# Shared network of a routed FFN in groups of four tiles: weights as the stationary operand of its first layer

## The chip, the cores and the metric

One core of a Trainium2 chip runs the kernel. The time is that of one execution on the device in microseconds (us), from the runs listed below. Five engines work side by side and meet at semaphores: the tensor engine (PE in the rows, PEld its weight loads), the vector engine (DVE), the scalar engine (ACT), GpSimd (POOL) and the sync engine (SP), which here only issues transfers. Each engine executes its own instructions in the order in which they are written.

## What is computed

The input is 64 x 64 rows of 512 values, 4096 tokens, seen as 32 tiles of 128. Each batch entry picks one of 8 matrices by a subject number; after that each token goes to 4 of 16 experts and to a shared network of the same form. Cut to what matters:

```
h      = einsum('bct,bcd->bdt', x, weights[subjects]) + bias[subjects]   # (64, 64, 512)
scores = sigmoid(h @ gate_weight.T)               # 16 experts, groups of 4, two best groups
w, sel = top 4 of the biased scores in those groups, weights normalised, times 2.5
out    = sum over the 4 experts of w * (silu(h @ g.T) * (h @ u.T)) @ d.T
shared = (silu(h @ shared_gate.T) * (h @ shared_up.T)) @ shared_down.T
return x + out + shared                           # H = 512, I = 256, float32
```

## The kernel before

**Stages.** A first stage, up to about 54 us, makes h, transposes it into kept_w and x_ring, computes the router's logits and starts the routing arithmetic. The shared stage then runs the shared network over the 32 tiles (steps 0 to 31); meanwhile the vector engine works out who goes where. The routed stage runs 143 tiles of gathered tokens (steps 32 to 174), each with one expert's weights, partly in loops of 16 steps. NT is 32, the first routed step.

**A step.** Products are made in float32 precision from two parts each, a high part rounded to the tensor engine's format and the low rest: three matmuls for each of four (first layer) or two (second layer) blocks of 128. In step n the tensor engine makes the first-layer product of tile n (`gate_up`, 12 matmuls of 512 columns, x stationary, the weights moving, gate and up side by side in one bank of psGU), transposes hid of tile n-1 (`xpose_hid`, 2 transposes to psH), and makes the second-layer product of tile n-2 (`down`, 6 matmuls to psY). Line 937 issues all the matmuls of products, line 814 all transposes.

The scalar engine copies y of tile n-3 (line 724), the high part of x of tile n+1 (`copy_xT`, 662), makes silu (772) and the high part of the transposed hid (717). The vector engine subtracts for the low part of x (`split_x`, 1385), multiplies silu and up (`mix`, 1408) and splits hid (1398).

**What lies between.** In the shared stage the vector engine carries pieces of the routing arithmetic, one or two for each step by the table ROUTE_STEPS (0 groups, 1 best groups, 2 top experts, 3 ties, 4 counts, ... 22 fill_idx), and the table entries by ENTRY_STEPS (16 entries in steps 10 to 20), which the scalar engine scales (`scale_lanes`, 757) and the tensor engine adds up in psM (`fill_slots`, 963, in the step behind). The tensor engine also makes a counting product in step 5 and word tables in step 14. HIGHS and LOWS say in which step the next experts' weights are split; GATHERS after which y the first gathers go out on GpSimd; RAW_LOADS the loads of weights.

The x of the shared stage is kept transposed. `shared_tile(n)` is the tile of step n, in x_ring for the first eight steps, in kept_w after them.

**The routed stage.** Steps 32 and on take x by gather, shuffle and a vector transpose (1392), two steps ahead. The vector and sync engines loop from step 48, the tensor and scalar engines from 46; DVE_HEAD fixes where the vector engine's loop body is loaded, and ACT_STEPS adds 52 semaphore instructions ahead of the scalar engine's code, which moves its loop body.

The functions that the diff touches follow.

## Time and profile before

| | us |
|---|---|
| median of 3 runs | 847.3 (845.91 to 850.49) |
| profiled execution | 847.83 |
| its span, first to last instruction | 846.1 |
| tensor engine busy | 824.8 (97%) |
| vector, scalar engine, GpSimd busy | 488.6 (58%), 406.9 (48%), 437.8 (52%) |
| granted clock of the tensor engine, mean | 0.995 |

A row of a timeline gives start, duration, engine, line, operation, what is written from what, shapes and a count; in brackets stands the idle time ahead of it and what ended that. Matmuls overlap, so what a matmul costs in a queue is the distance of the starts, not its duration.

### The profile page before, as it was taken

What the parts mean: (1) busy time and instruction counts of PE and PEld (TensorE: products, weight loads), DVE (VectorE), ACT (ScalarE), POOL (GpSimd) and SP (SyncE); (2) the same over time, 40 slices, a digit from 0 to 9 for tenths busy, and PEclk for the clock granted to TensorE, in tenths of its full rate; (3) what the DMA queues carried; (4) which work ended last, traced back from release to release, by engine and by line L of the source; (5) the groups of instructions that cost most, each with busy time, mean ns of one, the idle gap of its engine ahead of it and who ended that gap; (6) DMA issues with size and microseconds to landing.
All of it is one profiled execution on the core that took longest, in us unless ns stands there. A gap on an engine that the chain in (4) does not pass through costs nothing.

```text
span 846.1 us, 19696 instructions
## 1 busy us (share of the span) xinstructions
PE 824.8 (97%) x4200; PEld 660.7 (78%) x4201; DVE 488.6 (58%) x1016; ACT 406.9 (48%) x849; POOL 437.8 (52%) x400
## 2 busy tenths in 40 slices
PE   8999999999999999999999999999999999999994
PEld 5568878788888888788888888888888887887883
DVE  5688875645654455754457546646556566464441
ACT  4763457645444435534446435546455354453341
POOL 5403111265366556467565666655565675766433
PEclk9999999999999999999999999999999999999998
DMA  8977958599999999799997999798998998998744
GB/s 319 400 270 224 198 101 240 102 268 233 244 272 212 173 198 181 163 292 252 192 182 154 284 238 214 192 283 179 239 267 200 270 245 213 244 194 185 138 64 64
DMA packets 145307, 181.54 MB, mean 215 GB/s; under 512 B 30570, under 2 KB 103922, under 8 KB 142834
## 3 DMA queue, kind: packets, MB, share of 16 engines
q0 software_dynamic: 37776, 89.08, 51.7%
q1 hardware_dynamic: 106528, 80.45, 35.5%
q10 hardware_dynamic: 834, 10.49, 3.4%
q14 instruction: 151, 1.24, 0.5%
q8 instruction: 18, 0.29, 0.1%
HBM read 82.52 MB, written 67.17 MB: 177 GB/s over the span
## 4 chain that ended last, share of the span: by engine, by line
PE 85%; DMA 4%; DVE 3%; issue 3%; ACT 3%; DVEq 1%; ACTq 0%; SPq 0%; POOL 0%
PE psGU L937 53%; PE psY L937 26%; PE psH L814 4%; DMA h_rows<-tok_ring 3%; DVE xT_lo L1385 1%; ACT x_ring L757 1%; PE psM L963 1%; ACT tok_ring L670 1%; ACT xT_hi L662 0%; DVE x_ring L1367 0%; POOL out L594 0%; ACT y_ring L724 0%; DVEq L1490 0%; DMA cond_sb<-cond_w 0%; ACT x_ring L677 0%
## 5 line engine op out<-in xcount | busy, mean ns | idle before, releaser
L937 PE MATMUL psGU<-split_w,xT_hi 128*128 (+1 forms) x1400 | 433.9, 391 | 1.3 <-DVE xT_lo L1385 0.9
L594 POOL DMA_INDIRECT out<-y_ring,idx_all x143 | 235.3, 1646 | 207.4 <-SPq L485 189.4
L937 PEld LDWEIGHTS psGU<-split_w,xT_hi 128*128 128x128 f32 x1400 | 262.4, 188 | 59.1 <-issue 2.2
L937 PE MATMUL psGU<-split_w,xT_lo 128*128 (+1 forms) x700 | 273.8, 391 | 0.0
L937 PE MATMUL psY<-split_w,hidT_hi 128*128 (+1 forms) x700 | 233.2, 414 | 0.2 <-issue 0.2
L772 ACT ACTIVATE aT<-psGU 128x256 f32<-128x256 f32 x175 | 67.1, 384 | 263.6 <-PE psGU L937 208.8
L589 POOL DMA_INDIRECT tok_ring<-h_rows,idx_all x143 | 148.3, 1037 | 59.3 <-issue 43.1
L1385 DVE TENSOR_TENSOR xT_lo<-psT,xT_hi 128x512 fp32r<-128x512 f32 x143 | 98.7, 690 | 135.7 <-ACT xT_hi L662 101.3
L724 ACT ACTIVATE y_ring<-psY 128x512 f32<-128x512 f32 x174 | 103.1, 593 | 115.1 <-PE psY L937 88.6
L937 PEld LDWEIGHTS psGU<-split_w,xT_lo 128*128 128x128 f32 x700 | 131.4, 188 | 29.5
L937 PE MATMUL psY<-split_w,hidT_lo 128*128 (+1 forms) x350 | 138.2, 395 | 0.0
L937 PEld LDWEIGHTS psY<-split_w,hidT_hi 128*128 128x128 f32 x700 | 118.4, 189 | 17.0 <-issue 0.5
L1410 DVE SCALAR_TENSOR_TENSOR aT<-aT,w_ring,psGU 128x256 f32<-128x256 f32 x143 | 67.0, 468 | 93.9 <-ACT aT L772 65.4
L1392 DVE STREAM_TRANSPOSE psT<-x_ring 128x512 f32<-128x512 f32 x143 | 102.5, 717 | 4.6 <-issue 4.6
L602 POOL DMA_DIRECT2D out<-y_ring x32 | 29.1, 922 | 112.8 <-ACT y_ring L724 112.4
L662 ACT ACTIVATE xT_hi<-psT 128x512 fp32r<-128x512 f32 x143 | 84.8, 593 | 2.1 <-DVE psT L1392 2.1
L937 PEld LDWEIGHTS psY<-split_w,hidT_lo 128*128 128x128 f32 x350 | 65.6, 187 | 15.4
L1425 DVE TENSOR_TENSOR split_w<-raw_w,split_w x42 | 51.4, 1225 | 42.6 <-ACT split_w L734 29.2
L1398 DVE TENSOR_TENSOR hidT_lo<-psH,hidT_hi 128x256 fp32r<-128x256 f32 x175 | 72.7, 416 | 0.3
L814 PE MATMUL psH<-ident,aT 128*128 128x128 f32 x350 | 66.7, 272 | 1.3 <-DVE hidT_lo L1398 1.1
L814 PEld LDWEIGHTS psH<-ident,aT 128*128 128x128 f32 x350 | 48.0, 139 | 25.2 <-DVE aT L1410 1.6
L717 ACT ACTIVATE hidT_hi<-psH 128x256 fp32r<-128x256 f32 x175 | 66.5, 380 | 2.1 <-PE psH L814 1.7
(189 smaller groups left out, 403.4 us busy)
## 6 DMA issues: line engine op xcount, KB each, us to landing
x_ring<-tok_ring SPq DMA_DIRECT2D x284, 128.0 KB
raw_w<-ffn_w SPq DMA_DIRECT2D x17, 1536.0 KB, 10.4
h_rows<-tok_ring SPq DMA_DIRECT2D x32, 256.0 KB, 9.0
out<-y_ring POOLq DMA_DIRECT2D x32, 256.0 KB
x_ring<-x_pairs SPq DMA_DIRECT2D x12, 512.0 KB, 9.2
tok_ring<-h_rows,idx_all POOLq DMA_INDIRECT x143
out<-y_ring,idx_all POOLq DMA_INDIRECT x143
h_rows<-zeros POOLq DMA_DIRECT2D x1, 2112.0 KB, 9.1
```

What stands on the lines that cost most here:

```text
L589: pool.indirect_dma_start(tok_ring[:, r % RING, :], None, h_rows[:, :], bass.IndirectOffsetOnAxis(idx_all[:, r:r + 1], 0)).then_inc(gather ...
L594: pool.indirect_dma_start(out[:, :], bass.IndirectOffsetOnAxis(idx_all[:, r:r + 1], 0), y_ring[:, r % YRING, :], None, compute_op=ALU.add) ...
L662: act.activation(xT_hi[:, t.slot % 2, :], xT, ACT.Copy).then_inc(xhi_ready, 1)
L717: act.activation(hidT_hi[:, t.slot % 2, :], psH[:, 0:I], ACT.Copy).then_inc(hidhi_ready, 1)
L724: act.activation(y_ring[:, s, :], psY[t.slot % 2][:], ACT.Copy).then_inc(y_ready, 1)
L772: act.activation(silu[:, t.slot % 2, :], psGU[t.slot % 2][:, 0:I], ACT.Silu).then_inc(silu_ready, 1)
L814: mm = pe.transpose(dst[:, k * P:(k + 1) * P], src[:, k * P:(k + 1) * P], ident[:])
L937: mm = pe.matmul(dst, a[:, slot, c], w(at + col + k * H), start=(k == 0 and a is high and at == 0), stop=(k == parts - 1 and a is low))
L1385: v.tensor_tensor(xT_lo[:, t.slot % 2, :], xT, xT_hi[:, t.slot % 2, :].bitcast(F32), ALU.subtract).then_inc(xT_ready, 1)
L1392: v.transpose(psT[t.slot % 2][:].rearrange("p (k b j) -> p k j b", k=HK, j=QUADS), x_duo[:, t.slot // DUO_TILES, :, t.slot % DUO_TILES, :] ...
L1398: v.tensor_tensor(hidT_lo[:, t.slot % 2, :], psH[:, 0:I], hidT_hi[:, t.slot % 2, :].bitcast(F32), ALU.subtract).then_inc(hidT_ready, 1)
L1410: ins = v.scalar_tensor_tensor(out=hid[:, half, :], in0=gate, scalar=w_ring[:, w_slot, bass.ds(expert, 1)], in1=up, op0=ALU.mult, op1=ALU. ...
```

## The change

The shared stage runs in eight groups of four tiles. For one half c of the 256 inner columns (gate, then up) a product (`shared_product`) takes 128 columns of the weights as stationary operand and the four tiles' x as moving operand, four runs of 128 columns, so that hid comes out transposed, [inner, token]: 12 matmuls of 512 columns, gate to psGU[0], up to psGU[1], four products per group. Silu, mix, the high copy and the split of hid work on 512 columns for a half and four tiles. The second layer stays as it was, tile by tile (`shared_down`), one group behind. hid is not transposed there.

Buffers are found in others: high parts of x of a group in xT_pair, tok_ring or entry; low parts of x replace x in x_ring and kept_w; hid in aT and ties. New waits keep these apart (on gu_done for entries and gathers, on table_done and h_stored for copies). Steps 0 to 31 are written out ahead of the loops. The table of gathers, HIGHS and LOWS move; the padding on the scalar engine goes; in the routed stage the scalar engine copies y at the end of a step instead of at its start.

```diff
 KEPT_ORDER = [k * (KEPT // 2) + 2 * j + i for j in range(PIECES) for k in range(2) for i in range(2)]
-HIGHS = {18: (1, 0), 19: (1, 1), 20: (1, 2), 24: (2, 0), 28: (2, 1), 31: (2, 2)}
-LOWS = {21: ((1, 0),), 23: ((1, 1),), 24: ((1, 2),), 26: ((2, 0),), 29: ((2, 1),), 31: ((2, 2),)}
+HIGHS = {18: (1, 0), 19: (1, 1), 21: (1, 2), 25: (2, 0), 29: (2, 1), NT: (2, 2)}
+LOWS = {21: (1, 0), 23: (1, 1), 24: (1, 2), 26: (2, 0), 30: (2, 1), NT: (2, 2)}
+GROUP = 4
 RAW_LOADS = {15: 1, 16: 2, 23: 3, 31: 4}
 WARM_UP = 8
 DVE_HEAD = 77
...
 WEIGHTS_STORE = 3
-FIRST_GATHER = 20
-GATHERS = {20: (0, 1), 21: (2, 3), 22: (4, 5), 23: (6, 7), 25: (8, 9), 26: (10, 11), 27: (12, 13)}
+FIRST_GATHER = 18
+GATHERS = {18: (0, 1), 19: (2, 3, 4, 5), 20: (6, 7), 21: (8, 9), 22: (10, 11), 23: (12, 13)}
 
 
...
         aT = sb("aT", [P, 2, H])
-        xT_hi = sb("xT_hi", [P, 2, H], F32R)
-        xT_lo = sb("xT_lo", [P, 2, H], F32R)
+        xT_pair = sb("xT_pair", [P, GROUP, H], F32R)
+        xT_hi, xT_lo = xT_pair[:, 0:2, :], xT_pair[:, 2:4, :]
         silu, hid = aT[:, :, 0:I], aT[:, :, I:2 * I]
...
                 for r in GATHERS.get(n, ()):
+                    if r == RING - GROUP:
+                        pool.wait_ge(gu_done, NT - 2 * GROUP)
                     gather(r)
...
-            for _ in range(ACT_STEPS):
-                act.sem_inc(act_clear, 1)
...
+            def copy_shared_xT(n):
+
+                g, j = divmod(n, GROUP)
+                if n <= GROUP:
+                    act.wait_ge(a_xT_ready, NT if n == GROUP else shared_tile(n) + 1)
+                if n == GROUP:
+                    for k in range(RING - GROUP, RING):
+                        act.wait_ge(h_stored[k], 16 * (NT // RING))
+                if g >= 2 and j == 0:
+                    act.wait_ge(gu_done, GROUP * (g - 1))
+                if n == NT - GROUP:
+                    act.wait_ge(table_done, N_GROUPS)
+                act.activation(group_high(g)[:, j, :], kept_xT(shared_tile(n)), ACT.Copy).then_inc(xhi_ready, 1)
 
...
+            def shared_silu(g, c):
+
+                act.wait_ge(gu_done, GROUP * g + 2 * c + 1)
+                if c == 1 and g > 0:
+                    act.wait_ge(down_done, GROUP * g)
+                elif c == 0 and g > 1:
+                    act.wait_ge(down_done, GROUP * (g - 1))
+                act.activation(shared_hid(g, c), psGU[0][:], ACT.Silu).then_inc(silu_ready, 2)
+
+            def shared_hid_highs(g, c):
+
+                act.wait_ge(hid_ready, GROUP * g + 2 * c + 2)
+                act.activation(shared_hid_high(g, c), shared_hid(g, c), ACT.Copy).then_inc(hidhi_ready, 2)
+
...
+            def split_ahead(n):
+
+                turn, j = HIGHS[n]
+                if j == 0:
+                    act.wait_ge(raw_loaded, 16 * turn)
+                act.wait_ge(gu_done, KEPT_IN_X + (turn - 1) * KEPT + (j + 1) * GROUP)
+                split_high(turn, j)
+
+            def shared_step(n):
+
+                g, part = divmod(n, GROUP)
+                if part == 0 and g > 0:
+                    shared_hid_highs(g - 1, 1)
+                if n + GROUP < NT:
+                    copy_shared_xT(n + GROUP)
+                elif n == NT - 1:
+                    copy_xT(tile_at(NT), NT)
+                if part == 0:
+                    shared_silu(g, 0)
+                elif part == 1:
+                    shared_hid_highs(g, 0)
+                    if g > 0:
+                        shared_y(g - 1, 0)
+                elif part == 2 and g > 0:
+                    for j in range(1, GROUP):
+                        shared_y(g - 1, j)
+                for e in ENTRY_STEPS.get(n, ()):
+                    scale_lanes(e)
+                if part == 3:
+                    shared_silu(g, 1)
+                if n in HIGHS:
+                    split_ahead(n)
+                if n in X_COPIES:
+                    copy_x(X_COPIES[n])
 
             def next_weights(t, word):
...
             def step(t, n, j):
-                if n is None or n >= 3:
-                    copy_y(t + -3, None if n is None else n - 3)
-                if n is None or 0 < n < LAST:
+                if n == NT:
+                    shared_hid_highs(NT // GROUP - 1, 1)
+                if n is None or n < LAST:
                     copy_xT(t + 1, None if n is None else n + 1)
                 if n == NT:
                     act.wait_ge(words_ready, 1)
-                if not is_shared(n):
-                    word = act.value_load(act_word[0:1, bass.ds(t.done(-NT), 1)])
+                word = act.value_load(act_word[0:1, bass.ds(t.done(-NT), 1)])
                 act.wait_ge(gu_done, t.done(1))
-                if n is None or n >= 2:
-                    act.wait_ge(hid_ready, t.done(-1))
+                act.wait_ge(hid_ready, t.done(-1))
                 act.activation(silu[:, t.slot % 2, :], psGU[t.slot % 2][:, 0:I], ACT.Silu
                                ).then_inc(silu_ready, 1)
-                if n != 0:
+                if n == NT:
+                    for k in range(GROUP):
+                        shared_y(NT // GROUP - 1, k)
+                    split_ahead(NT)
+                else:
                     copy_hidT(t + -1, None if n is None else n - 1)
-                for g in ENTRY_STEPS.get(n, ()):
-                    scale_lanes(g)
-                if not is_shared(n):
-                    next_weights(t, word)
-                elif n in HIGHS:
-                    turn, j = HIGHS[n]
-                    if j == 0:
-                        act.wait_ge(raw_loaded, 16 * turn)
-                    act.wait_ge(xT_ready, KEPT_IN_X + (turn - 1) * KEPT + (j + 1) * (KEPT // PIECES))
-                    split_high(turn, j)
-                if n in X_COPIES:
-                    copy_x(X_COPIES[n])
+                    if n is None or n >= NT + 3:
+                        copy_y(t + -3, None if n is None else n - 3)
+                next_weights(t, word)
 
             act.activation(warm[:], ones[:, 0:1], ACT.Silu)
+            for n in range(NT):
+                shared_step(n)
             run_tiles(act, *FFN, step)
...
+            def shared_product(g, c, up):
+
+                col = up * I + c * P
+                for k in range(HK):
+                    high, low = group_high(g)[:, :, k * P:(k + 1) * P], group_low(g, k)
+                    in_four = psGU[up][:].rearrange("p (t q) -> p t q", q=P)
+                    as_low = in_four if len(low.shape) == 3 else psGU[up][:].rearrange("p (a i q) -> p a i q", a=2, q=P)
+                    w = k * H + col
+                    pe.matmul(in_four, split_w[:, w:w + P], high, start=(k == 0), stop=False)
+                    pe.matmul(as_low, split_w[:, w:w + P], low, start=False, stop=False)
+                    mm = pe.matmul(in_four, split_w[:, EW + w:EW + w + P], high, start=False, stop=(k == HK - 1))
+                return mm
+
+            def shared_down(g, j):
+
+                n = GROUP * g + j
                 if j == 0:
-                    kept.clear()
-                if n == NT:
-                    pe.wait_ge(words_ready, 1)
-                elif n == 1:
-                    pe.wait_ge(scored, LOGIT_GROUPS)
-                at, needed = weights(t, n)
-                kept.append(at)
-                gate_up(t, n, kept[-1], needed)
-                if n != 0:
-                    xpose_hid(t + -1, None if n is None else n - 1)
+                    pe.wait_ge(hidT_ready, GROUP * (g + 1))
+                if n >= 2:
+                    pe.wait_ge(y_ready, n - 1)
+                token = slice(j * P, (j + 1) * P)
+                for c in range(IK):
+                    low = shared_hid_low(g, c)
+                    for a, at in ((shared_hid_high(g, c), 0), (shared_hid_high(g, c), EW), (low, 0)):
+                        w = at + UP + c * H
+                        mm = pe.matmul(psY[n % 2][:], a[:, token], split_w[:, w:w + H], start=(c == 0 and a is not low and at == 0),
+                                       stop=(c == IK - 1 and a is low))
+                mm.then_inc(down_done, 1)
+
+            def shared_step(n):
+
+                g, part = divmod(n, GROUP)
+                if part == 0:
+                    pe.wait_ge(xT_ready, GROUP * (g + 1))
+                    if g > 0:
+                        pe.wait_ge(silu_ready, GROUP * g)
+                    shared_product(g, 0, 0).then_inc(gu_done, 1)
+                elif part == 1:
+                    if g > 0:
+                        pe.wait_ge(hid_ready, GROUP * g)
+                    shared_product(g, 0, 1).then_inc(gu_done, 1)
+                    if g > 0:
+                        shared_down(g - 1, 0)
+                elif part == 2:
+                    if g > 0:
+                        for j in range(1, GROUP):
+                            shared_down(g - 1, j)
+                else:
+                    pe.wait_ge(silu_ready, GROUP * g + 2)
+                    shared_product(g, 1, 0).then_inc(gu_done, 1)
+                    pe.wait_ge(hid_ready, GROUP * g + 2)
+                    shared_product(g, 1, 1).then_inc(gu_done, 1)
                 if n in PE_POS_FFN:
                     positions(PE_POS_FFN[n])
                 elif n == PE_WORDS:
                     word_tables()
                 elif n == PE_SP_WORDS:
                     sp_table()
-                if is_shared(n):
-                    for g in ENTRY_STEPS.get(n - 1, ()):
-                        fill_slots(g)
-                if n is None or n >= 2:
+                for e in ENTRY_STEPS.get(n - 1, ()):
+                    fill_slots(e)
+
+            pe.wait_ge(h_ready, NT)
+            pe.wait_ge(low_done, PIECES)
+            for n in range(NT):
+                shared_step(n)
+            pe.wait_ge(scored, LOGIT_GROUPS)
+            pe.sem_inc(hid_xposed, NT)
+            pe.wait_ge(words_ready, 1)
+            kept = []
+
+            def step(t, n, j):
+                if j == 0:
+                    kept.clear()
+                at, needed = weights(t, n)
+                kept.append(at)
+                gate_up(t, n, kept[-1], needed)
+                if n == NT:
+                    for k in range(GROUP):
+                        shared_down(NT // GROUP - 1, k)
+                else:
+                    xpose_hid(t + -1, None if n is None else n - 1)
+                if n is None or n >= NT + 2:
                     down(t + -2, None if n is None else n - 2,
...
+            def split_shared_x(n):
+
+                g, j = divmod(n, GROUP)
+                if n == 0:
+                    v.wait_ge(logits_done, LOGIT_GROUPS - 1)
+                elif n == GROUP:
+                    v.wait_ge(logits_done, LOGIT_GROUPS)
+                v.wait_ge(xhi_ready, n + 1)
+                tile = shared_tile(n)
+                v.tensor_tensor(low_xT(tile), kept_xT(tile), group_high(g)[:, j, :].bitcast(F32),
+                                ALU.subtract).then_inc(xT_ready, 1)
+
+            def shared_mix(g, c):
+
+                v.wait_ge(silu_ready, GROUP * g + 2 * c + 2)
+                v.wait_ge(gu_done, GROUP * g + 2 * c + 2)
+                hid_c = shared_hid(g, c)
+                v.tensor_tensor(hid_c, hid_c, psGU[1][:], ALU.mult).then_inc(hid_ready, 2)
+
+            def split_shared_hid(g, c):
+
+                v.wait_ge(hidhi_ready, GROUP * g + 2 * c + 2)
+                hid_c = shared_hid(g, c)
+                v.tensor_tensor(shared_hid_low(g, c), hid_c, shared_hid_high(g, c).bitcast(F32), ALU.subtract
+                                ).then_inc(hidT_ready, 2)
+
+            def shared_step(n):
+
+                g, part = divmod(n, GROUP)
+                if part == 0 and g > 0:
+                    shared_mix(g - 1, 1)
+                elif part == 2:
+                    split_shared_hid(g, 0)
+                    if g < NT // GROUP - 1:
+                        split_shared_x(GROUP * (g + 1))
+                route_part(n)
+                if part == 0 and g > 0:
+                    split_shared_hid(g - 1, 1)
+                elif part == 1:
+                    shared_mix(g, 0)
+                elif part >= 2 and g < NT // GROUP - 1:
+                    for j in ((1,) if part == 2 else (2, 3)):
+                        split_shared_x(GROUP * (g + 1) + j)
+                if n in LOWS:
+                    split_low(*LOWS[n])
+                if n == NT - 2:
+                    turn_x(tile_at(NT))
+                elif n == NT - 1:
+                    split_x(tile_at(NT))
+                    turn_x(tile_at(NT + 1))
...
-            split_x(tile_at(0), 0)
+            for n in range(GROUP):
+                split_shared_x(n)
             route_weights(0)
             def copy_y(t):
```

**On the vector engine**, between best groups and ties of the routing arithmetic. `aT` takes mix, `hidT_lo` or `aT_low` the split of hid, `xT_lo` or `x_low` the split of x, MAX is top experts. Before:

```order
L1408 TENSOR_TENSOR aT<-aT,psGU 128x256
L1398 TENSOR_TENSOR hidT_lo<-psH,hidT_hi 128x256
L1385 TENSOR_TENSOR xT_lo<-x_ring,xT_hi 128x512
L1120 MAX top<-masked 128x8 x16
L1019 TENSOR_TENSOR ties<-masked,top 128x16x16
```

Now:

```order
L1576 TENSOR_TENSOR aT<-aT,psGU 128x512
L1582 TENSOR_TENSOR aT_low<-aT,hidT_hi 128x512
L1568 TENSOR_TENSOR x_low<-x_ring,tok_high 128x512
L1290 MAX top<-masked 128x8 x16
L1189 TENSOR_TENSOR ties<-masked,top 128x16x16
```

Mix and split of hid now serve four tiles and stand once in two steps; the splits of x that the next group needs (tiles 4 to 7) stand one here, one behind top experts and two behind ties.

**On the tensor engine**, where a first-layer product is followed by a second-layer one (before: steps 2 and 3; now: steps 4 and 5). `psGU` is the first layer, `psY` the second, `psH` the transposed hid. Before:

```order
L937 MATMUL psGU<-split_w,xT_lo 128x512
L814 MATMUL psH<-ident,aT 128x128 x2
L937 MATMUL psY<-split_w,hidT_hi 128x512 x2
L937 MATMUL psY<-split_w,hidT_lo 128x512
L937 MATMUL psY<-split_w,hidT_hi 128x512 x2
```

Now:

```order
L1091 MATMUL psGU<-x_low,split_w 128x512
L1092 MATMUL psGU<-tok_high,split_w 128x512
L1107 MATMUL psY<-split_w,hidT_hi 128x512 x2
L1107 MATMUL psY<-split_w,aT_low 128x512
L1107 MATMUL psY<-split_w,hidT_lo 128x512 x2
```

The two transposes are gone, and x has become the moving operand of psGU; the product to psY has the six matmuls that it had.

**On the scalar engine**, around the first table entries (steps 10 and 11). L757 and L876 are the scaling of entries. Before:

```order
L662 ACTIVATE xT_hi<-kept_w 128x512
L772 ACTIVATE aT<-psGU 128x256
L717 ACTIVATE hidT_hi<-psH 128x256
L757 ACTIVATE x_ring<-x_ring,token_no 128x512 x2
L724 ACTIVATE y_ring<-psY 128x512
```

Now:

```order
L790 ACTIVATE y_ring<-psY 128x512 x3
L876 ACTIVATE x_ring<-x_ring,token_no 128x512 x2
L727 ACTIVATE tok_high<-kept_w 128x512
L876 ACTIVATE x_ring<-x_ring,token_no 128x512 x2
L799 ACTIVATE aT<-psGU 128x512
```

Three copies of y stand together, and a silu of the group (L799) stands behind two scalings of entries.

## Rows read from the trace of the kernel before

**Rows 1.** The page: busy time by engine, and the group of the transposes.

```profile
PE 824.8 (97%) x4200; PEld 660.7 (78%) x4201; DVE 488.6 (58%) x1016; ACT 406.9 (48%) x849; POOL 437.8 (52%) x400
...
L814 PE MATMUL psH<-ident,aT 128*128 128x128 f32 x350 | 66.7, 272 | 1.3 <-DVE hidT_lo L1398 1.1
```

**Rows 2.** Timeline, tensor engine: stage's start, one step, first routed products.

```profile
54.25 0.70 PE L937 MATMUL psGU<-split_w,xT_hi 128*128 128x512 f32 x2
...
62.92 0.71 PE L937 MATMUL psY<-split_w,hidT_hi 128*128 128x512 f32 x2
...
64.39 0.62 PE L937 MATMUL psGU<-split_w,xT_hi 128*128 128x512 f32 x2
...
67.13 0.38 PE L814 MATMUL psH<-ident,aT 128*128 128x128 f32 x2
67.27 0.71 PE L937 MATMUL psY<-split_w,hidT_hi 128*128 128x512 f32 x2
...
205.70 0.62 PE L937 MATMUL psGU<-split_w,xT_hi 128*128 x2
...
214.41 0.62 PE L937 MATMUL psGU<-split_w,xT_hi 128*128 x2
```

**Rows 3.** Tensor engine: first matmuls of steps 5, 6, 14, 15, 19, 20.

```profile
73.10 0.62 PE L937 MATMUL psGU<-split_w,xT_hi 128*128 128x512 f32 x2
...
78.53 0.62 PE L937 MATMUL psGU<-split_w,xT_hi 128*128 128x512 f32 x2
...
116.05 0.62 PE L937 MATMUL psGU<-split_w,xT_hi 128*128 128x512 f32 x2
...
122.76 0.62 PE L937 MATMUL psGU<-split_w,xT_hi 128*128 128x512 f32 x2
...
144.61 0.62 PE L937 MATMUL psGU<-split_w,xT_hi 128*128 128x512 f32 x2
...
150.03 0.62 PE L937 MATMUL psGU<-split_w,xT_hi 128*128 128x512 f32 x2
```

**Rows 4.** Timeline, vector engine: route weights, groups and best groups.

```profile
51.65 0.42 DVE L1019 TENSOR_TENSOR w_num<-raw_w,scores 128x256 f32<-128x256 f32 x1
...
53.72 0.68 DVE L1385 TENSOR_TENSOR xT_lo<-x_ring,xT_hi 128x512 fp32r<-128x512 f32 x1
54.78 0.43 DVE L1019 TENSOR_TENSOR masked<-scores,ebias 128x256 f32<-128x256 f32 x1 [0.38 <-ACT scores L682]
...
56.02 0.55 DVE L1097 TENSOR_REDUCE group_sum<-raw_w 128x64 f32<-128x384 f32 x1
...
58.83 0.41 DVE L1019 TENSOR_TENSOR beats<-group_sum 128x48 f32<-128x48 f32 x3
...
61.21 0.42 DVE L1408 TENSOR_TENSOR aT<-aT,psGU 128x256 f32<-128x256 f32 x1
```

**Rows 5.** Timeline, vector engine: a split of x, top experts and ties.

```profile
61.88 0.68 DVE L1385 TENSOR_TENSOR xT_lo<-x_ring,xT_hi 128x512 fp32r<-128x512 f32 x1
62.48 1.32 DVE L1120 MAX8 top<-masked 128x8 f32<-128x16 f32 x16
...
65.35 0.42 DVE L1408 TENSOR_TENSOR aT<-aT,psGU 128x256 f32<-128x256 f32 x1
...
66.62 1.33 DVE L1019 TENSOR_TENSOR ties<-ties 128x256 f32<-128x256 f32 x3
...
69.37 0.42 DVE L1408 TENSOR_TENSOR aT<-aT,psGU 128x256 f32<-128x256 f32 x1
```

**Rows 6.** Timeline, scalar engine: copies of x, scalings, a routed step's silu.

```profile
50.31 1.15 ACT L662 ACTIVATE xT_hi<-x_ring 128x512 fp32r<-128x512 f32 x2 [0.27 <-issue]
...
143.57 2.61 ACT L757 ACTIVATE x_ring<-x_ring,token_no 128x512 f16<-128x512 f16 x4 [0.79 <-DVE x_ring L1367]
...
771.27 0.38 ACT L772 ACTIVATE aT<-psGU 128x256 f32<-128x256 f32 x1 [1.66 <-PE psGU L937]
```

**Rows 7.** Timeline, vector engine, where its loop ends.

```profile
779.25 0.73 DVE L1392 STREAM_TRANSPOSE psT<-x_ring 128x512 f32<-128x512 f32 x1 [4.56 <-issue]
```

133 lines of the change are left out of this document (84 added, 49 removed).

## The prediction

> **What bounds the kernel now.** I read the page first, then the tensor engine's instructions in order of time, then the vector and scalar engines over the same stretch. The tensor engine is busy for 824.8 of 846.1 us and no other engine for more than 58% [rows 1]. So a microsecond is gained only where the tensor engine executes less or waits less, and lost where it waits more. The profiled execution took 847.83 us, 0.5 above the median of 847.3; sums are made against it and 0.5 is taken off at the end.
>
> The change touches the shared stage: from the first product at 54.25 us to the first routed product at 205.70, and the two steps behind it, where the last second-layer products of the stage drain [rows 2]. By 214.41 both orders have done the same work: 34 first-layer products, 32 second-layer products. I compare how long that takes, 160.16 us now.
>
> A plain step [rows 2] is a first-layer product (12 matmuls, 64.39 to 67.13 = 2.74), a pair of transposes of hid (0.14), and a second-layer product (6 matmuls, 62.92 to 64.39 = 1.47), 4.35 from 62.92 to 67.27. The other work sits between steps, priced as a step's period less 4.35 [rows 3]: second counting product 5.43 - 4.35 = 1.08; word tables 6.71 - 4.35 = 2.36 (I take 2.3); two table fills 5.42 - 4.35 = 1.07, so 0.56 for one. There are 16 fills, 6 pairs and 4 single (8.7); the small word table I put at 0.6. Sum 12.6.
>
> **Part 1, transposes removed.** 64 transposes in 32 pairs. The page lists them at 272 ns each [rows 1], but that is latency. A pair advances the queue 0.14, and the second-layer product behind it begins with 0.55 for two matmuls instead of 0.46, hence 1.47 instead of 1.38. So a pair is worth 4.35 - 2.74 - 1.38 = 0.23, and 32 pairs 7.4 us. By the Trainium skill, page TensorE: Matmul & The Clock Gate, section Part 4: PE-mode transpose, a 128x128 transpose takes about 275 ns in a kernel; the trace's duration agrees (272), but as time in the queue that would be 64 x 0.275 = 17.6 us, and the spacing here says 7.4. I use the spacing.
>
> **Part 2, the first layer turned round.** Per group of four tiles 4 products of 12 matmuls of 512 columns: 48, as before. The moving operand is now four runs of 128 columns instead of one of 512. No row shows this form for these types. The nearest, the table fills, move every second f16 element of 144, 16 matmuls in 1.07 us [rows 3], 67 ns each with their transitions, or 0.46 ns per column against 227 / 512 = 0.44 for plain ones. I take zero; 384 matmuls make 1.9 us of each 5 ns, above only, since nothing in a gather of runs can be quicker than a plain stream.
>
> **Part 3, vector and scalar work.** The same elements in half as many instructions for hid (512 wide). A 512-wide vector operation advances its queue 0.60 (61.88 to 62.48) [rows 5], a 512-wide scalar one 0.53 (two in 1.15 less the tail) [rows 6]. That is cheaper in total than before, and off the bound. What is not off it is where these instructions stand: a group cannot start until all four of its tiles are split, where before one split sufficed, and the routing arithmetic is still queued between them in the same places.
>
> I walk the queues group by group with those prices; a group of the tensor engine is 4 x 2.74 + 4 x 1.38 = 16.48.
>
> Start: two more scalar copies (0.53 each) fit before the last logits copy, and the fourth split stands about where the second stands now, 53.72 to 54.40 [rows 4]; I let the first product start at 54.5 (+0.25).
>
> Group 0 has no second layer: 10.96, ready for group 1 at 65.5. The vector queue from 54.4 [rows 4, 5]: route weights 2.07 (51.65 to 53.72), groups 1.79 (54.78 to 56.57), best groups 2.38 (58.83 to 61.21), mix 0.61, a 0.85 wait for the scalar copy of hid (0.62 = 1.15 - 0.53 [rows 6], the tail of mix and the signals), split of hid 0.61, split of tile 4 0.60, top experts 2.87 (62.48 to 65.35), split of tile 5 0.60, ties 2.75 (66.62 to 69.37), splits of tiles 6 and 7 1.2. Sum 16.4: the queue reaches the end at 70.8. Group 1 starts at 70.9: **a wait of 5.4 us**, the largest new term. Before, the same arithmetic lay inside four steps of which each needed one split.
>
> Group 1 ends at 70.9 + 16.48 + 1.08 = 88.5. By the same kind of sum its splits for group 2 end 0.9 ahead of that, those for group 3 only 0.4 ahead. The further waits are estimates, each between zero and one piece of routing arithmetic (2.87 [rows 5]), and I name what is late. In group 2 the third second-layer product needs a bank of y whose copy stands, on the scalar engine, behind the copy of hid, which waits for mix, which stands behind top slots on the vector engine: 0.7. At its end the silu stands behind the scaling of a late table entry: 0.4. So group 2 ends at 88.5 + 16.48 + 0.7 + 0.56 (a fill) = 106.2 and group 3 starts at 106.6. Group 3: + 16.48 + two single fills and a pair 2.19 + word tables 2.3 + 0.6 = 128.2. Group 4: + 16.48 + a single fill and three pairs 3.77, and four scalings in 2.61 [rows 6] stand ahead of the copies of y (0.6) and again of the last silu (0.4): group 5 starts at 149.4 and ends, + 16.48 + two pairs 2.14, at 168.0. Groups 6 and 7 have nothing beside them: 201.0. Then the first routed product, four second-layer products, the second routed product and its transposes, 2.74 + 5.52 + 2.74 + 0.23 = 11.23, and a wait of 0.8, since the next tile's high copy stands behind four copies of y and a weight split: 213.0.
>
> Sum: 213.0 against 214.41, a gain of 1.4. Put otherwise: 7.4 from the transposes; the present stage holds 160.16 - (34 x 2.74 + 32 x 1.38 + 33 x 0.23 + 12.6) = 2.7 of waits that mostly go, because second-layer products now cover the fills; less 8.3 of new waits and 0.25 at the start; rounding makes the rest. From there the routed stage runs the same loops at 4.35 a tile [rows 2], so the gain is carried to the end: 847.8 - 1.4 = 846.4, less 0.5: **845.9 us**. The gathers move two tiles earlier in the table; the tensor engine does not wait for them now, and the first transposes that need them stand at step 30, 40 us behind. I put them at nothing; without that cover a gather and its shuffle would show.
>
> **Rivals.**
> 1. The vector queue does not hold up group 1 (less than half of the waits come true). For it: the rows' spacings include small waits between dependent operations, and a margin of one microsecond decides several of the smaller terms. Against: 16.4 us of listed work against 10.96. With no new wait at all: 846.4 - 8.3 - 0.5 = 837.6; with half, 841.7.
> 2. Slower: the routed loops. The change takes 52 padding instructions off the scalar engine's stream and many real ones from it, so its loop body lies elsewhere; the vector engine's loop keeps its fixed place. What a badly placed jump costs is seen on the vector engine: 4.56 us of idle with nothing to wait for, where its loop ends [rows 7]. The scalar engine has 1.66 us in hand in each step [rows 6], so it decides from a stall above that. Such a stall at loop entry and exit costs 2 x (4.56 - 1.66) = 5.8: 851.7; at all eight turns and the exit, 26, 872. By the Trainium skill, page Runtime: NRT & Kernel Launch, section Instruction fetch mechanics, a taken branch whose target is not in the two blocks held forces a fetch; the 4.56 us agrees with it, and no row tells where the new scalar loop falls.
> 3. Split matmuls slower: at 10% (23 ns) each, 384 x 0.023 = 8.8: 854.7. Against it the fills above. It would have to be above 4 ns to eat the forecast gain.
> 4. The longer queues make more waits than I walked: the splits for groups 2 and 3 come 0.9 and 0.4 us ahead only. Two more microseconds: 848.
>
> **How the numbers follow.** Forecast with its near neighbours (rival 4 too), 843 to 850: 0.65. Rival 1: 0.22. Rival 2: 0.09. Rival 3: 0.04. The forecast's time is the predicted one. The range takes in half of the way to rival 1's end and rival 2's smaller price: 839.5 to 851.5. A measurement tells 0.5%, 4.2 us, from no change: faster means below 843.1 (rival 1 and a little of the forecast's edge), slower above 851.5 (rivals 2 and 3).
>
> **What would show it.** The tensor engine idle for about 5 us before the second group's first product, waiting for the vector engine's split of x, shows the main term; its absence shows rival 1. The group's first product four times 2.74 after the start shows part 2; longer spacing rival 3. A period of 4.10 per tile in groups 6 and 7 shows part 1; 4.35 would mean that the transposes cost nothing. Idle time on the scalar engine above 1.7 us at the loop's turns shows rival 2. The forecast is wrong if the routing arithmetic on the vector engine is faster in the new order than its rows say, or if the routed stage's period is no longer 4.35.

## The result, and the profile after

The changed kernel takes 854.19 us (median of 19 runs, 852.70 to 858.74), the kernel before, run beside it, 848.80 (19 runs). The ratio is 1.0076, with a 95% interval of 1.0062 to 1.0091: slower by 5.4 us. The forecast was 845.9 and the range ended at 851.5. In the profiled executions the span grew from 846.1 to 851.8 us.

The page and the timeline of the tensor engine after, in groups that answer to [rows 1] and [rows 2]. The columns are those of the rows ahead; L1090 to L1092 are the three matmuls of a group's product, L1107 the second-layer products of the shared stage, L1049 the routed products.

```profile
span 851.8 us, 19349 instructions
PE 822.1 (97%) x4136; PEld 655.7 (77%) x4137; DVE 488.1 (57%) x984; ACT 391.8 (46%) x817; POOL 435.4 (51%) x400
```

```profile
54.29 0.47 PE L1090 MATMUL psGU<-xT_pair,split_w 128*128 128x512 f32 x1
...
65.06 0.39 PE L1092 MATMUL psGU<-xT_pair,split_w 128*128 128x512 f32 x1
70.70 0.80 PE L1090 MATMUL psGU<-tok_high,split_w 128*128 128x512 f32 x1 [5.26 <-DVE x_low L1568]
...
92.07 0.50 PE L1090 MATMUL psGU<-xT_pair,split_w 128*128 128x512 f32 x1 [0.93 <-DVE split_w L1568]
...
110.14 0.47 PE L1090 MATMUL psGU<-tok_high,split_w 128*128 128x512 f32 x1 [0.45 <-ACT aT L799]
132.04 0.48 PE L1090 MATMUL psGU<-xT_pair,split_w 128*128 128x512 f32 x1
...
205.41 2.92 PE L1049 MATMUL psGU<-split_w,xT_pair 128*128 x12
208.99 0.96 PE L1107 MATMUL psY<-split_w,ties_low 128*128 128x512 f32 x3 [0.65 <-DVE aT_low L1582]
220.69 3.01 PE L1049 MATMUL psGU<-split_w,xT_pair 128*128 x12 [2.92 <-DVE split_w L1642]
```

The tensor engine is busy 2.7 us less than in [rows 1] (822.1 against 824.8) and the span is 5.7 longer: it waits more. The piece of work that took 160.16 us in [rows 2], from the first product to the first-layer product of tile 34, now takes 220.69 - 54.29 = 166.40.

How the tensor engine's clock went around the first long wait. Each row is a stretch: its length, busy times and counts of PE, PEld, DVE, ACT and POOL, then the granted clock as a share of full speed, DMA share and GB/s.

```profile
60.00:65.40 5.40, 5.40 (x25) 4.17 (x23) 4.42 (x23) 2.25 (x4) 0.00 (x0) 1.00 0.53 194
65.40:70.70 5.30, 0.05 (x1) 0.00 (x0) 5.05 (x12) 0.00 (x0) 0.00 (x0) 0.86 0.00 0
70.70:76.00 5.30, 5.29 (x13) 4.14 (x14) 4.93 (x13) 1.15 (x2) 0.00 (x0) 0.50 0.00 0
76.00:81.50 5.50, 5.50 (x26) 4.57 (x25) 2.15 (x5) 2.73 (x5) 0.18 (x1) 1.00 0.00 0
```

During the 5.26 us of waiting the clock fell to one half (1.2 of 2.4 GHz), and the first 12 matmuls of group 1 ran at it: they took from 70.70 to 75.99, 5.29 us instead of 2.74. That cost 2.55 us in this execution, which no step of the prediction holds.

The second place is the end of the stage. The scalar engine, and then the vector engine, ahead of the wait of 2.92:

```profile
210.68 0.60 ACT L790 ACTIVATE y_ring<-psY 128x512 f32<-128x512 f32 x1 [1.92 <-PE psY L1107]
...
214.86 0.60 ACT L790 ACTIVATE y_ring<-psY 128x512 f32<-128x512 f32 x1 [0.80 <-PE psY L1107]
215.35 1.05 ACT L708 ACTIVATE split_w<-raw_w 128x1024 fp32r<-128x1024 f32 x1
216.30 1.05 ACT L853 ACTIVATE split_w<-raw_w  x1
217.26 0.58 ACT L713 ACTIVATE xT_pair<-psT 128x512 fp32r<-128x512 f32 x1
```

```profile
216.44 1.23 DVE L1244 TENSOR_TENSOR split_w<-raw_w,split_w 128x1024 fp32r<-128x1024 f32 x1 [6.52 <-ACT split_w L708]
218.60 1.23 DVE L1642 TENSOR_TENSOR split_w<-raw_w,split_w  x1 [0.94 <-DVE split_w L1244]
219.75 0.69 DVE L1556 TENSOR_TENSOR xT_pair<-psT,xT_pair 128x512 fp32r<-128x512 f32 x1
```

At step 32 the scalar engine writes the four y of group 7 first, each a second-layer product apart (210.68 to 214.86), and only then the high part of the last shared weight split (L708) and of the next expert's (L853). The vector engine's low parts (L1244, L1642) wait for these, and its split of x for tile 34 stands in its queue behind both: it starts at 219.75. The profile names L1642 as releaser; the product needs the split behind it.

**Where the 5.7 us went**, by the spans: the stage + 6.24; from the product of tile 34 to the scalar engine's last silu - 1.15 (614.10 against 615.25); from there to the issue of the last scatter + 1.25 (7.92 against 6.67); from that to the end - 0.63; the start + 0.04. The 1.15 is no merit of the change's products: in the kernel before, the routed step that starts at 777.03 takes 6.10 us instead of 4.35, behind the vector engine's standstill of 4.56 [rows 7], and after, where that standstill is 2.08, no step there is lengthened (one at 699.8 takes 5.72). The + 1.25 shows in these rows, first of the kernel after, then of before: the last copy of hid on the scalar engine comes 3.15 us after the instruction ahead of it, against 1.34.

```profile
839.09 0.38 ACT L783 ACTIVATE hidT_hi<-psH 128x256 fp32r<-128x256 f32 x1 [3.15 <-PE psY L1049]
```

```profile
831.66 0.38 ACT L717 ACTIVATE hidT_hi<-psH 128x256 fp32r<-128x256 f32 x1 [1.34 <-PE psH L814]
```

### The profile page after: what moved, and what is told of

Same layout as the page of the kernel before. It is cut to its first block, busy times and chain, and to the rows that moved or that the text cites. A ratio compares the mean times of both kernels' runs of the same rounds, so it can differ in the third digit from the quotient of the medians.

```text
span 851.8 us, 19349 instructions
## 1 busy us (share of the span) xinstructions
PE 822.1 (97%) x4136; PEld 655.7 (77%) x4137; DVE 488.1 (57%) x984; ACT 391.8 (46%) x817; POOL 435.4 (51%) x400
## 4 chain that ended last, share of the span: by engine, by line
PE 83%; DVE 2%; issue 1%; ACT 1%; ACTq 0%; DVEq 0%; POOL 0%; SPq 0%
PE psGU L1049 45%; PE psY L1049 23%; PE psH L928 4%; PE psY L1107 3%; PE psGU L1090 2%; PE psGU L1092 2%; PE psGU L1091 2%; PE psM L1077 1%; ACT x_ring L876 0%; DVE aT L1576 0%; PE psT L1013 0%; POOL out L650 0%; DVE entry L1537 0%; DVE aT_low L1582 0%; DVE split_w L1642 0%
## 5 line engine op out<-in xcount | busy, mean ns | idle before, releaser
L1049 PE MATMUL psGU<-split_w,xT_pair 128*128 x1716 | 415.9, 391 | 4.1 <-DVE split_w L1642 2.9
L1049 PEld LDWEIGHTS psGU<-split_w,xT_pair 128*128 128x128 f32 x1716 | 321.9, 188 | 75.1 <-issue 5.4
L1049 PE MATMUL psY<-split_w,hidT_hi 128*128 x572 | 190.6, 414 | 1.7 <-DVE hidT_lo L1620 1.5
L1556 DVE TENSOR_TENSOR xT_pair<-psT,xT_pair 128x512 fp32r<-128x512 f32 x143 | 98.8, 691 | 64.5 <-ACT xT_pair L713 49.0
L1049 PE MATMUL psY<-split_w,hidT_lo 128*128 x286 | 113.0, 395 | 0.0
L1049 PEld LDWEIGHTS psY<-split_w,hidT_hi 128*128 128x128 f32 x572 | 96.8, 189 | 15.9 <-issue 2.4
L713 ACT ACTIVATE xT_pair<-psT 128x512 fp32r<-128x512 f32 x143 | 86.5, 605 | 5.3 <-DVE psT L1614 3.1
L1642 DVE TENSOR_TENSOR split_w<-raw_w,split_w x42 | 51.5, 1226 | 43.4 <-ACT split_w L853 41.6
L1049 PEld LDWEIGHTS psY<-split_w,hidT_lo 128*128 128x128 f32 x286 | 53.6, 187 | 12.6
L1620 DVE TENSOR_TENSOR hidT_lo<-psH,hidT_hi 128x256 fp32r<-128x256 f32 x143 | 59.6, 417 | 2.4 <-ACT hidT_hi L783 2.4
L928 PE MATMUL psH<-ident,aT 128*128 128x128 f32 x286 | 54.4, 272 | 0.0
L853 ACT ACTIVATE split_w<-raw_w x42 | 44.8, 1066 | 0.9 <-issue 0.2
L1091 PE MATMUL psGU<-split_w 128*128 128x512 f32 x96 | 37.6, 391 | 0.0
```

Source lines behind the costliest of these rows:

```text
L713: act.activation(xT_hi[:, t.slot % 2, :], psT[t.slot % 2][:], ACT.Copy).then_inc(xhi_ready, 1)
L928: mm = pe.transpose(dst[:, k * P:(k + 1) * P], src[:, k * P:(k + 1) * P], ident[:])
L1049: mm = pe.matmul(dst, a[:, slot, c], w(at + col + k * H), start=(k == 0 and a is high and at == 0), stop=(k == parts - 1 and a is low))
L1091: pe.matmul(as_low, split_w[:, w:w + P], low, start=False, stop=False)
L1556: v.tensor_tensor(xT_lo[:, t.slot % 2, :], psT[t.slot % 2][:], xT_hi[:, t.slot % 2, :].bitcast(F32), ALU.subtract).then_inc(xT_ready, 1)
L1620: v.tensor_tensor(hidT_lo[:, t.slot % 2, :], psH[:, 0:I], hidT_hi[:, t.slot % 2, :].bitcast(F32), ALU.subtract).then_inc(hidT_ready, 1)
```

## The experiments

All are edits of the changed kernel unless said otherwise. "Stage" is the time from the first product to the product of tile 34: 160.16 before, 166.40 after. The medians of the kernel before in the runs' company were 848.5 to 848.8. The intervals of e1 to e6 and of e9 still meet that of the kernel after (1.0062 to 1.0091); for these the traces say more than the medians.

**e1: keep the tensor engine busy in the first wait.**

```
+                if n == GROUP:
+                    for k in range(23):
+                        pe.matmul(psY[0][:], split_w[:, 0:P], split_w[:, 0:H], start=True, stop=True)
```

> The changed kernel with 23 extra matmuls of 512 columns (5.2 us of work, results unused, into a bank of psY that is free then) on the tensor engine ahead of its wait for the first product of group 1. Theory (the wait for the vector engine's splits of x costs 5.3 us, and the tensor engine's clock, which fell to half behind it, costs another 2.6): the first product of group 1 starts at 70.7 as in the changed kernel, but with a granted clock of 1.00, so that its 12 matmuls are 0.23 apart instead of 0.43; the kernel is 2.6 us faster than the changed one, about 851.6. Rival (the loss lies in the routed stage, or in the form of the new matmuls): no change or slower, 854 and above.

Measured: 852.43 us, 1.0057 [1.0032, 1.0083]; stage 164.0. The stretch behind the wait, and the filler itself:

```profile
65.98 5.38 PE L1116 MATMUL psY<-split_w 128*128 128x512 f32 x23
71.45 0.50 PE L1090 MATMUL psGU<-tok_high,split_w 128*128 128x512 f32 x1
```

```profile
71.00:76.00 5.00, 4.91 (x22) 3.73 (x21) 4.74 (x11) 2.27 (x4) 0.00 (x0) 1.00 0.00 0
```

The clock stays at full and the stage is 2.4 us shorter, although the group starts no earlier. So these 2.4 us were the clock's. The median fell by 1.8 only; how much half clock follows this wait differs from run to run, as the last section shows. By the Trainium skill, page TensorE: Matmul & The Clock Gate, section Part 1: The HAM clock gate, the engine's clock is halved, to 1.2 GHz, once it has been idle for a while; the trace agrees (0.50 behind the wait of 5.26 us), and this rule, read against the forecast wait of 5.4, speaks for a group that starts at half speed.

**e2 and e9: the hand-over at step 32.** In e2 the weight split (split_ahead) goes ahead of the four copies of y; in e9 the next expert's weights go between them as well, as here:

```
...
                 if n == NT:
-                    for k in range(GROUP):
-                        shared_y(NT // GROUP - 1, k)
-                    split_ahead(NT)
+                    split_ahead(NT)
+                    for k in range(GROUP - 2):
+                        shared_y(NT // GROUP - 1, k)
+                    next_weights(t, word)
+                    for k in range(GROUP - 2, GROUP):
+                        shared_y(NT // GROUP - 1, k)
+                    return
...
```

> The changed kernel with the weight split of step 32 on the scalar engine ahead of the four copies of y instead of behind them. Theory (the wait of 2.9 us at step 34 comes from the vector engine's weight splits, which stand ahead of its split of x and wait for the scalar engine's high parts behind the copies of y): the shared part of that wait goes, but the next expert's first piece still stands behind the copies, so 0.5 to 2.4 us faster than the changed kernel, 852 to 853.7. Rival (the wait is the loops' or the transfers'): no change, 854.2.

> The changed kernel with the scalar engine's weight split of step 32, and the next expert's first pieces, ahead of the third copy of y instead of behind the fourth; nothing else. Theory: of the 2.9 us that the tensor engine waits at step 34 at least 1.9 go (0.95 went when only the first of the two was moved): 2 us faster than the changed kernel, 852. Rival: the wait passes to another place of the same step, no change.

Measured: e2 853.42, 1.0059 [1.0042, 1.0076], the wait ahead of tile 34 1.95 instead of 2.92. e9 852.83, 1.0047 [1.0029, 1.0064], that wait gone (the product starts right behind the transposes). So the whole wait hangs on the order of one engine's queue at one step. The median fell by 1.4 us, less than the wait of 2.92: the step behind tile 34 starts 4.76 us after it instead of 4.46, and e9's execution had a wait of 1.73 at 747.72 in the routed stage that the kernel after has smaller (1.15 at 705.50).

**e3 and e4: less work, or other work, ahead of group 1.** e3 moves the route weights from ahead of step 0 to step 12 (and their store with them); e4 takes the splits of tiles 5, 6, 7 ahead of the routing pieces between them:

```
-            route_weights(0)                  # e3, ahead of step 0
+                if n == 12:
+                    route_weights(0)
-WEIGHTS_STORE = 3
+WEIGHTS_STORE = 12
...
-                        split_shared_x(GROUP * (g + 1))      # e4
+                        for j in range(GROUP if g == 0 else 1):
+                            split_shared_x(GROUP * (g + 1) + j)
...
-                elif part >= 2 and g < NT // GROUP - 1:
+                elif part >= 2 and 0 < g < NT // GROUP - 1:
```

> The changed kernel with the first half of the route weights (2.07 us of vector work) moved from ahead of step 0 to step 12, and the store of the weights from y 3 to y 12. Theory (vector queue too long for group 0): group 1 starts 2.1 us earlier, the wait ahead of it is 3.2 us; if the clock still falls, 2.1 us faster than the changed kernel (852.1), if a wait of 3.2 us leaves it, 4.7 us faster (849.5). Rival (something other than the vector queue releases group 1): the start of group 1 stays at 70.7 and the time at 854.2.

> The changed kernel with the splits of x of tiles 4 to 7 all ahead of top experts and ties on the vector engine. Nothing is taken away, only the order. Theory: group 1 starts at about 65.4 without a wait; mix of group 0's second half now stands behind top experts and ties, so that the second product of group 1 waits about 3 us for it. The sum of waits falls by 2 to 2.5 us, and if a wait of 3 us leaves the clock, the 2.6 us of half clock go too: 849.5 to 852. Rival (the amount of vector work and not its order decides, since the queue is full up to group 2): no change, 854.

Measured: e3 857.39 us, 1.0112 [1.0068, 1.0156], slower by 3 instead of faster. The wait ahead of group 1 shrank by 0.26 only (to 5.00) although 2.07 us of vector work was gone, because the vector engine now waits itself, for the product that it mixes:

```profile
61.57 0.69 DVE L1576 TENSOR_TENSOR aT<-aT,psGU 128x512 f32<-128x512 f32 x1 [1.41 <-PE psGU L1092]
63.09 0.69 DVE L1582 TENSOR_TENSOR aT_low<-aT,hidT_hi 128x512 fp32r<-128x512 f32 x1 [0.83 <-ACT hidT_hi L804]
```

What sets group 1's start is therefore not all the work since 54.4, as the prediction summed it, but the chain from the end of the first pair of products: mix, copy of hid, split of hid, then the routing pieces and the splits. The 3 us came at the other end: from the last scatter's issue to the end e3 takes 12.4 us, against 9.1 after. (The first product also came 1.4 us later in this execution, at 55.71.)

e4 856.61, 1.0094 [1.0059, 1.0130]. The wait at group 1's start is gone and stands 12 matmuls later, and a second one has doubled:

```profile
71.19 0.50 PE L1090 MATMUL psGU<-tok_high,split_w 128*128 128x512 f32 x1 [3.11 <-DVE aT L1576]
...
89.99 0.50 PE L1090 MATMUL psGU<-xT_pair,split_w 128*128 128x512 f32 x1 [2.02 <-DVE split_w L1568]
...
220.14 5.48 PE L1049 MATMUL psGU<-split_w,xT_pair 128*128 x12 [2.91 <-DVE split_w L1643]
```

Moving splits alone moves the wait (to the mix that now stands behind the routing), since the vector engine has too much to do in groups 0 and 1 as long as the routing pieces stay in these steps. The last row shows the clock at half again, behind the same 2.9 us as above, where the kernel after kept full speed. The clock was also lowered behind the wait of 3.11 and, with no wait, behind the word tables (0.82 from 122.0 to 131.5), which is part of why e4 is no faster than the kernel after.

**e5: the transposes back.** 31 pairs of transposes of zeros into a bank that nobody reads, one in each step.

```
+                if n >= 1:
+                    transposes(psH, zeros, IK)
```

> The changed kernel with two transposes per step put back into the shared stage (31 pairs, of a constant tile into psH, results unused). Theory: they cost their place in the queue, 0.23 us a pair wherever the tensor engine is the bound, 29 pairs of them outside the wait ahead of group 1, so about 6.7 us slower than the changed kernel, 861; the period of a group in the second half of the stage goes from 16.5 to 17.4. Rival A (their listed duration counts): 31 x 2 x 0.272 = 17 us, 871. Rival B (they are hidden under their neighbours): no change, 854.

Measured: 858.57, 1.0107 [1.0090, 1.0124], 4.4 above the kernel after; the stage is 2.8 longer, 169.2. All waits shrank (5.26 to 4.54, 0.93 to 0.49, 0.45 and 0.25 to none, 0.65 to 0.43). Where nothing waits, in groups 6 and 7, a group takes 17.45 and 17.48 us against 16.62 and 16.65 after, 0.21 for each pair. So the removal gives something, but a part of the 7.4 us of saved transposes was only exchanged for waits.

The clock fell here too behind the first wait, for a shorter time than after: the 12 matmuls behind it took 4.44 us, 1.7 more than at full speed instead of 2.55. At the same clock the stages would differ by 3.7.

```profile
70.93 0.50 PE L1090 MATMUL psGU<-tok_high,split_w 128*128 128x512 f32 x1 [4.54 <-DVE x_low L1572]
...
75.37 0.38 PE L928 MATMUL psH<-ident,zeros 128*128 128x128 f32 x2
```

```profile
70.90:75.50 4.60, 4.57 (x14) 3.58 (x15) 4.34 (x10) 1.15 (x2) 0.00 (x0) 0.63 0.00 0
```

**e6: the routed y copy back at the step's start.** The prediction passed over this move of one copy.

```
+                if n is None or n >= NT + 3:
+                    copy_y(t + -3, None if n is None else n - 3)
                 if n is None or n < LAST:
                     copy_xT(t + 1, None if n is None else n + 1)
```

> The changed kernel with the copy of y at the start of a routed step again, as in the kernel before, instead of at its end. Theory (the routed stage is bound by the tensor engine either way, 631.1 us from the third routed product to the end against 631.7 before): within 1 us of the changed kernel, 853 to 855. Rival (the new place delays the scatter or the high copies and is part of the loss): 2 us or more faster, below 852.

Measured: 854.52, 1.0059 [1.0043, 1.0076]: no difference from the kernel after that these runs can tell.

**e8, e13, e11: another timetable.** If the miss is work in the wrong place, a timetable that keeps the vector engine free at the start must give it back. e8 moves the routing pieces later, in the table of steps and with it the table entries, gathers, raw loads and weight splits that depend on it; takes the first splits ahead; gives group 1 a hid buffer of its own; holds e3's and e9's edits. The core of it:

```
+ROUTE_STEPS = {0: ("groups",), 1: ("best_groups",), 4: ("top_experts",), 6: ("ties",), 7: ("counts",), 8: ("weights",),
+               9: ("ranks",), 10: ("take_turns", "starts"), 11: ("slots", "keys"), 12: ("top_slots",), 13: ("places",),
+               14: ("words",), 15: ("columns",), 17: ("tables",), 19: ("read_words",), 25: ("fill_idx",),
```

> The changed kernel with the routing arithmetic moved behind the splits that the next group needs: top experts to step 4, ties 6, counts 7, ranks 9, and so on to tables 17, entries in steps 14 to 23, fill_idx 25, first gather behind y 21; the splits of x of tiles 4 to 7 directly behind the split of hid; hid of group 1 in a free part of tok_ring, since ties are now written later; and in step 32 the weight splits of the scalar engine between the copies of y. No work is added or left out. Theory: group 1 starts at 65.5 without a wait and without the fall of the clock, group 2 without its 0.9 us, and the wait of 2.9 at step 34 falls to about 1: 5.3 + 2.6 + 0.9 + 1.9 = 10.7 us less than the changed kernel, 843.5, faster than the kernel before (848.8) by 5. Rival (the moved arithmetic makes waits later in the stage, or the late gathers and weight splits hold up the routed stage): 848 or more.

Measured: 850.68, 1.0022 [1.0007, 1.0036], 7 above what was expected. The stage is 159.65, 6.75 shorter than after and a little shorter than before. Left are waits of 0.85 (101.24), 1.60 (120.74) and 2.35 us (166.66, with half clock behind it), the latter two for a silu that stands behind scalings of table entries; and the end is 12.9 us instead of 9.1. e13 takes back e3's part alone:

> e8_resched with the expert weights of the tokens and their store alone back where they are in after (one change out of the four of e11_order). If the store's place in GpSimd's stream made the longer end of e3 and e8 (12.4 and 12.9 us after the last scatter's issue, 9.1 to 9.8 in the others): the end is 9.5 and the time about 848, 3 under e8, unless the weights' 2.1 us on VectorE ahead of step 0 come back in the stage (then 849 to 850). If not: 850.7, as e8.

Measured: 845.72, 0.9974 [0.9957, 0.9991], 5 us under e8; from the last scatter's issue to the end 9.8 instead of 12.9, and the spans differ by 4.5, of which the stage has 0.8 and its start 0.7. The weights and their store at step 12 or 13 lengthen the end, in e3 as in e8; by which way no run tells: the last transfers end about 5 us behind that issue in both, and e8 then takes 3 us more in which no engine does anything.

e11 is e13 with three swaps of neighbours in a queue:

```
+                if part == 3:                     # scalar engine: silu ahead of the scalings
+                    shared_silu(g, 1)
                 for e in ENTRY_STEPS.get(n, ()):
                     scale_lanes(e)
...
+                elif part == 3 and 0 < g < NT // GROUP - 1:   # vector engine: splits ahead of routing
+                    for j in (2, 3):
+                        split_shared_x(GROUP * (g + 1) + j)
                 route_part(n)
...
+                if n == NT:                       # vector engine, step 32: hid ahead of x
+                    split_shared_hid(NT // GROUP - 1, 1)
                 if n is None or n < LAST:
                     split_x(t + 1)
```

> The kernel e8_resched, changed in four places: the expert weights of the tokens and their store by GpSimd are back where they are in after; ScalarE writes the second silu of a group ahead of the scaling of entries of that step; VectorE takes the splits of x of the fourth part of a group ahead of the routing piece; at step 32 it splits the second half of hid of group 7 ahead of the split of x. Theory: the waits of e8 of 0.85, 1.60, 2.35 (with 1.7 of half clock behind it) and 0.65 go, so the stage takes 153 instead of 159.65, and the end after the last scatter is 9.5 instead of 12.9 because the store is back. Then 840 to 844, ratio 0.990 to 0.995. Rival: what is taken ahead pushes the entries, and the wait moves to the gathers or to the word tables; then the stage takes 158 or more and the time is 848 or above. Rival on the end: it stays at 12.9, then the store is not its cause.

Measured: 841.21 us, 0.9913 [0.9889, 0.9937], under the kernel before by 7 us, with the change's own group products. The kernel before was not run with this timetable; e16 below is the nearest to it. Its tensor engine, the only wait of the stage among the rows, and the product of tile 34 (starting at 208.54):

```profile
54.88 0.47 PE L1100 MATMUL psGU<-xT_pair,split_w 128*128 128x512 f32 x1
...
197.29 2.98 PE L1059 MATMUL psGU<-split_w,xT_pair 128*128 x12 [0.43 <-DVE xT_pair L1566]
...
208.54 3.00 PE L1059 MATMUL psGU<-split_w,xT_pair 128*128 x12
```

The stage takes 153.66, where 153 was expected.

**e16: the transposes back where nothing waits.** e5's edit on e11.

> e11_order with the 31 pairs of transposes of e5_transposes_back back in the stage (of zeros, into a bank that nobody reads), as the change's part alone where nothing else waits. Theory: with no wait left in the stage each pair costs its full 0.23, 7.1 in all: 848 to 849, ratio 1.000; in e5, where waits covered part, 2.8 to 4.4 were seen. Rival (the pairs give the other engines time, and TensorE waits elsewhere anyway): 843 to 845.

Measured: 847.76, 0.9989 [0.9973, 1.0005], 6.5 above e11, where e5 cost 4.4. The spans differ by 4.6, the stages by 4.0 (157.63). A pair among the matmuls, which are 0.23 apart elsewhere:

```profile
95.64 0.40 PE L1117 MATMUL psY<-split_w,aT_low 128*128 128x512 f32 x1
95.88 0.38 PE L938 MATMUL psH<-ident,zeros 128*128 128x128 f32 x2
96.01 0.48 PE L1100 MATMUL psGU<-xT_pair,split_w 128*128 128x512 f32 x1
96.33 0.39 PE L1101 MATMUL psGU<-split_w 128*128 128x512 f32 x1
```

From 95.64 to 96.33 there are two matmuls and the pair: 0.69 - 2 x 0.227 = 0.24 for the pair, the price of part 1; the medians give 0.21, 6.5 for 31. What the stages differ by is less, because e11's profiled execution lost 1.8 us to the clock from 132 us on, behind the word tables (small products of 16 rows), which e16's did not, and waited 0.43. First the two stretches of e11, then the second of e12 (below), whose program is e11's in this stage:

```profile
123.80:132.00 8.20, 8.20 (x50) 5.98 (x49) 5.73 (x9) 4.69 (x9) 3.44 (x4) 1.00 0.62 154
132.00:147.80 15.80, 15.80 (x88) 12.43 (x87) 9.01 (x15) 9.56 (x17) 0.00 (x0) 0.89 0.83 246
```

```profile
132.00:147.80 15.80, 15.80 (x97) 12.44 (x95) 9.70 (x16) 10.09 (x18) 0.01 (x1) 1.00 0.79 240
```

e12 kept full clock there and waited nowhere: its stage takes 151.37, and e16's 157.63 is 6.26 above it, 0.20 for each of the 31 pairs.

**e10, e12, e15: the 52 empty increments.** The diff removes 52 semaphore increments of the scalar engine that stand ahead of its loop and do nothing. e10 is the kernel after with them, e12 is e11 with them, e15 the kernel before without.

```
+            for _ in range(ACT_STEPS):
+                act.sem_inc(act_clear, 1)
```

> The kernel after with the 52 empty semaphore increments of ScalarE put back ahead of its loop, and nothing else. Theory A (the lines removed there shifted ScalarE's code, and so placed a stall at its loop's exit): the silu-to-split row behind the last gate_up products falls from the 3.15 us wait of after towards the 0.5 of before, the time is 1 to 2 us under that of after, near 852.5, ratio to before 1.004 to 1.006; the stage up to gate_up(34) stays at 166.4. Theory B (that wait is no matter of code, but of the order of work in the last routed steps): nothing moves, 854, ratio 1.0075.

> e11_order with the 52 empty increments of ScalarE back as well. By the theory of code placement 1 to 2 us under e11_order, 839 to 843; otherwise equal to e11_order.

> The kernel before without the 52 empty semaphore increments of ScalarE. e10_pads showed stalls of 3.5 to 6.6 us of ScalarE's x copy every 72 us once they are put ahead of the changed kernel's loop. Theory (what counts is where the loop's code comes to lie, and 52 was the count that suited the old code): without them the old kernel shows such stalls at its loop's turns, 855 to 875. Rival (the increments cost by being there, whatever the code behind them): the old kernel is as fast or faster without, 845 to 849.

Measured: e10 874.17, 1.0311 [1.0284, 1.0337], 20 us above the kernel after; e12 858.25, 1.0121 [1.0093, 1.0149], 17 above e11; e15 853.11, 1.0066 [1.0040, 1.0092], 4.6 above the kernel before. Both expectations of a small gain were wrong. In e10 the scalar engine stands still with nothing to wait for, about every 72 us, a turn of the loop, and the tensor engine pays with waits and with the clock:

```profile
420.19 0.60 ACT L715 ACTIVATE xT_pair<-psT 128x512 fp32r<-128x512 f32 x1 [4.84 <-issue]
```

```profile
421.69 2.99 PE L1051 MATMUL psGU<-split_w,xT_pair 128*128 x12 [1.56 <-DVE xT_pair L1558]
494.04 4.54 PE L1051 MATMUL psGU<-split_w,xT_pair 128*128 x12 [2.44 <-DVE xT_pair L1558]
568.75 4.60 PE L1051 MATMUL psGU<-split_w,xT_pair 128*128 x12 [3.32 <-DVE xT_pair L1558]
```

The page's row for that copy, in e10 and in the kernel after (last column: idle ahead of it and its chief cause):

```profile
L715 ACT ACTIVATE xT_pair<-psT 128x512 fp32r<-128x512 f32 x143 | 86.6, 606 | 52.4 <-issue 39.9
```

```profile
L713 ACT ACTIVATE xT_pair<-psT 128x512 fp32r<-128x512 f32 x143 | 86.5, 605 | 5.3 <-DVE psT L1614 3.1
```

In e15 the same kind of row stands in the old loop:

```profile
552.61 0.60 ACT L724 ACTIVATE y_ring<-psY 128x512 f32<-128x512 f32 x1 [3.52 <-issue]
```

So the increments are good for one code and bad for the other, and the standing rows wait for nothing: what is left as the cause is where the code behind them comes to lie (no row shows the loading of code itself). Taking them out was a needed part of the change, worth 20 us with the new loop. In one thing e10 is better than the kernel after: its last copy of hid waits 0.86 instead of 3.15. So that stall at the loop's exit moves with the increments too, and is probably of the same kind; e8, e11 and e13, also without them, are as short there as e10 (7.0 us from the last silu to the last scatter's issue).

**e14: the two missed terms together.** e1's and e9's edits.

> The two terms that the prediction missed, taken away together: the 23 filler matmuls of e1_busy ahead of group 1 (its output is the reference's), and ScalarE's order of e9_nw at step 32. Theory (the clock behind the first wait, and the late split ahead of gate_up(34) with the half clock behind it, are separate costs and make most of the miss): the gains add, 2 from the one and 1.4 from the other (by the medians against after), up to 2.6 and 4.3 by the traces; 848.5 to 851, ratio 1.000 to 1.003. Rival (they share a cause, or what one gives is taken back by the other's wait): 852.5, ratio 1.005, as either alone.

Measured: 850.96, 1.0031 [1.0011, 1.0051]. Against the kernel after 3.2 less, where e1 gave 1.8 and e9 1.4: the medians add as separate costs would, and this sum is clear of the noise (the intervals do not touch). In the trace the stage is 160.8 (55.31 to 216.15), 5.6 shorter than after and as long as before; the span is 2.8 shorter, since the first product came 1.0 later in this execution, the routed steps took 1.3 more, and the end took 0.65 more.

## Why the prediction was wrong

By its own steps; times are starts on the tensor engine in us.

| step | forecast | measured |
|---|---|---|
| first product | 54.5 | 54.29 |
| group 1 | 70.9, after 5.4 of wait | 70.70, after 5.26 |
| group 2 | 88.5 | 92.07 |
| group 3 | 106.6 | 110.14 |
| group 4 | 128.2 | 132.04 |
| group 6 | 168.0 | 172.14 |
| first routed product | 201.0 | 205.41 |
| product of tile 34 | 213.0 | 220.69 |

- **The wait ahead of group 1** was the largest term and right to 0.2 us. The reading behind it was partly wrong: e3 showed that only the chain behind the first products counts. The sum came out because in this order the vector engine reaches the mix just when the product is ready.
- **The step that failed first** is "Group 1 ends at 70.9 + 16.48 + 1.08 = 88.5". It prices every matmul behind a wait of 5.4 us at full speed. The clock fell, and group 1 took 2.55 us more; e1 took that away and gained 2.4 in the stage, 1.8 in the median. The kernel before had no long wait of the tensor engine in this stage, so its rows price no matmul behind one. A case "the wait halves the clock" should have stood among the rivals.
- **"Its splits for group 2 end 0.9 ahead"** was wrong by 1.8 us: the wait was 0.93. The 0.4 ahead of group 3 came true (0.45); the others of groups 2 and 4 were smaller than forecast, 0.25 at 143.92 the only one above 0.2. From group 2 to the first routed product the forecast needed 112.5 us and 113.34 were taken. The difference is nearly all in groups 3, 5 and 7 (0.3, 0.3 and 0.2), whose moving operand lies in tok_high or entry_high, with the four tiles further apart or in another buffer than in xT_pair: their matmuls are 0.2325 apart instead of 0.2275, about 0.9 us in the 192 of groups 1, 3, 5 and 7. That it fits so well is partly luck, since smaller waits made up for second-layer products that took a little more than their 1.38. Part 2's zero was thus close, within its bound of 5 ns each, and rival 3 is out.
- **"A wait of 0.8"** ahead of tile 34 is the second term that was mis-sized: 2.92, and 0.65 ahead of the second-layer products in group 7's drain that was not forecast. The prediction named the right queue ("behind four copies of y and a weight split") but followed it on the scalar engine alone. On the vector engine two weight splits, each waiting for the scalar engine's, stand ahead of the split of x. e9 and e14 took the wait away.
- **Part 1** was near in its price of 0.23 a pair: 0.24 in e16's rows, 0.20 and 0.21 over whole stages and groups. Groups 6 and 7 took 16.62 and 16.65 us, 4.16 a tile, against 4.35 before and the 4.10 that was to show part 1. Of the page's 272 ns a transpose only the spacing is time in the queue. But the saving could not arrive in the changed kernel, which waited in its stead (e5: the wait ahead of group 1 shrank by 0.72 for the three pairs put back ahead of it).
- **Rival 2** named the padding. It saw the danger in taking it out; in truth that was necessary (e10) and left a stall at the exit alone, part of 1.25 us. The other side, 20 us, was within what it priced for all eight turns (26). Its 1.66 us in hand does not hold for the new loop: behind the standstills of 4.84, 5.72 and 6.59 us in e10 the tensor engine waited 1.56, 2.44 and 3.32, each 3.3 less.
- **The routed stage**, taken as unchanged, took 1.15 less up to the last silu and 1.25 more behind it.
- **The range** has two slips, neither of which saves it: half of the way to rival 1's end is 841.7 and not 839.5, and rival 2's smaller price, 851.7, lies just outside the 851.5 that was to take it in.

The terms from forecast to measurement, up to tile 34: clock 2.55, group 2's wait 0.93, operand form 0.9, waits at the hand-over 2.8, start - 0.2; together 7.0 of 7.7. The gain of 1.4 became a loss of 6.3 by the start of tile 34. Without the two chief terms e14 comes to 851.0, still 5.1 above the forecast. Of these, 2.3 lie in the stage (160.8 against 158.5: the wait of group 2, the operand form, the wait of 0.65), 1.0 at the exit (7.70 against 6.67), 0.8 in a first product later than forecast (55.31 against 54.5), and the rest in what lies between span and median (2.0 here, 1.2 in the forecast).

## What to carry to other kernels

When work is grouped so that one engine starts only after several pieces of another's, walk every queue that feeds it up to the last piece, and put the feeding pieces ahead of work that nobody waits for: the same change was 5 us slower in the old timetable and, with a new one, 7 us faster than the kernel before (e11), about what its transposes are worth there (e16). A wait of some microseconds on the engine that sets the time must be priced with the slower clock behind it, here 1.5 to 2.55 us. And padding that places loop code belongs to the code behind it: measure it again, with and without, whenever that code changes.

## What the hardware did that was not expected

- The tensor engine's clock fell to half behind the first wait in every run that had it, but not for equally long. At full speed the first 12 matmuls of group 1 take 2.74 us. Behind waits of 5.0 to 5.3 us they took 5.29 (the kernel after, e2), 5.25 (e3), 4.68 (e9), 4.31 (e6) and 4.22 (e10), and behind 4.54 us in e5 4.44. e6 and e10 have the program of the kernel after up to there but for the increments at the start, so the difference is the execution's: the same wait cost 1.5 to 2.55 us of clock.
- Behind 2.9 us of waiting for tile 34 the 12 matmuls took 3.01 to 3.03 us in the kernel after, e1 and e3, but 4.39, 4.60, 4.61 and 5.48 in e5, e6, e10 and e4. So the length of the last wait alone does not tell it either.
- The clock also fell with no wait at all, behind 2.1 us of products of 16 rows, in e11 (0.89 over 15.8 us) and in e4 (0.82 over 9.5 us), and not in e12 and e16. e12 has e11's program in this stage, so it is not the transposes of e16 that kept the clock up.
- 52 empty instructions ahead of a loop moved the kernel by + 20, + 17 and - 4.6 us, according to the code behind them (the last is the kernel before, faster with them), through standstills of mostly 3 to 6.6 us at the loop's turns. By the Trainium skill, page Runtime: NRT & Kernel Launch, section Instruction fetch mechanics, a taken branch to code that is not held forces a fetch; these rows agree with that, though none shows a fetch.
